# A graph network on one core: the dense rows by products of the layers' weights, on a periodic schedule, with beta added by VectorE

## The reference

```python
h = relu(layernorm(x))
x = x + L0(h)            # (h + aggregated messages) @ W0.T + b0, leaky 0.01
h = relu(layernorm(x))
x = x + L1(h)            # four attention layers, each as below
# one layer: h = x @ W; out = segment_sum(h[src] * alpha, dst) + b
#   mu, var over the row; x = (out - mu) * rsqrt(var + eps) * g + beta
```

## Time and profile before

| | |
|---|---|
| median of 3 runs | 3483.99 us (3440.52 to 3486.61) |
| profiled execution | 3488.22 us, its span 3486.5 us |
| busy share of the span | PE 64%, DVE 62%, ACT 49%, POOL 40% |
| mean granted TensorE clock | 0.677 of full |
| data moved by DMA | 126.29 MB, mean 36 GB/s |

### The profile page before, as it was taken

The page is one execution under the profiler, slowest core; times in us unless marked ns, Lnnn a source line. Parts: engine busy times, 40 slices in busy tenths (PEclk is TensorE's granted clock), DMA queues, the critical chain, the costliest instruction groups (busy, mean ns, idle before and its releaser), DMA issues. The chain is left out here.

```text
span 3486.5 us, 45031 instructions
## 1 busy us (share of the span) xinstructions
PE 2234.9 (64%) x11717; PEld 1789.5 (51%) x11717; DVE 2147.7 (62%) x8249; ACT 1723.3 (49%) x5173; POOL 1377.2 (40%) x1089
## 2 busy tenths in 40 slices
PE   2788888886546488890288891188894088797000
PEld 2666666664334366780166781166683066686000
DVE  2367776666888567448767448777446867412880
ACT  0265665554557556444566444566445456422340
POOL 5588778670112466000366000266100076200367
PEclk9976775565555566995567895566697566678555
DMA  6221222110002311000311000311000311003011
GB/s 123 59 50 32 45 67 55 31 19 15 0 0 79 102 34 26 16 1 0 107 34 26 16 1 0 106 34 26 17 1 1 96 26 42 18 1 71 3 31 37
DMA packets 101670, 126.29 MB, mean 36 GB/s; under 512 B 59443, under 2 KB 67563, under 8 KB 98091
## 3 DMA queue, kind: packets, MB, share of 16 engines
q1 hardware_dynamic: 38634, 97.42, 9.8%
q0 software_dynamic: 62400, 25.68, 4.4%
q10 hardware_dynamic: 432, 0.79, 0.1%
HBM read 78.68 MB, written 64.50 MB: 41 GB/s over the span
## 5 line engine op out<-in xcount | busy, mean ns | idle before, releaser
L227 POOL DMA_INDIRECT S<-row_t,INFG x400 | 516.5, 1291 | 1101.1 <-issue 1101.1
L221 PE MATMUL bank<-WC,XT 128*125 128x128 f32 x4800 | 845.9, 330 | 0.0
L221 PEld LDWEIGHTS bank<-WC,XT 128*125 128x125 f32 x4800 | 712.6, 227 | 172.7 <-issue 172.7
L210 PE MATMUL bank<-ident,Y 125*128 125x125 f32 x2200 | 443.7, 354 | 434.1 <-ACT Y L708 396.3
L210 PEld LDWEIGHTS bank<-ident,Y 125*128 125x128 f32 x2200 | 355.0, 189 | 481.1 <-issue 394.1
L217 PE MATMUL bank<-BR,ones 3*125 3x512 bf16 x725 | 385.1, 531 | 125.9 <-ACT XT L697 75.7
L735 DVE TENSOR_REDUCE ss<-Y 125x4 f32<-125x512 f32 x300 | 205.6, 685 | 367.6 <-ACT Y L680 367.6
L221 PE MATMUL bank<-W,XT 128*125 128x128 f32 x1200 | 310.4, 438 | 44.2 <-ACT XT L1033 44.2
L697 ACT ACTIVATE XT<-bank,BC,GC 128x500 f32<-128x500 f32 x300 | 230.3, 768 | 185.7 <-PE bank L210 185.7
L221 PEld LDWEIGHTS bank<-W,XT 128*125 128x125 f32 x1200 | 265.8, 326 | 108.5 <-issue 54.6
L217 PEld LDWEIGHTS bank<-BR,ones 3*125 3x125 bf16 x725 | 107.1, 148 | 273.8 <-ACT XT L697 118.9
(11 more groups left out here) (205 smaller groups left out, 3961.8 us busy)
## 6 DMA issues: line engine op xcount, KB each, us to landing
R<-in_x SPq DMA_DIRECT2D x100, 224.0 KB
out_rows<-R SPq DMA_DIRECT2D x100, 224.0 KB
row_t<-T SPq DMA_DIRECT2D x20, 1120.0 KB
S<-row_t,INFG POOLq DMA_INDIRECT x400
R<-in_edge_attr SPq DMA_DIRECT2D x1, 5600.0 KB
x_t<-R SPq DMA_DIRECT2D x5, 1120.0 KB
S<-x_t SPq DMA_DIRECT2D x1, 5600.0 KB
R<-in_x SPq DMA_DIRECT2D x100, 26.0 KB
```

The lines of the kernel that those rows point to most:

```text
L210: ins = nc.tensor.transpose(ps[:, a * P:(a + 1) * P], t, ident[0:P, 0:P])
L221: ins = nc.tensor.matmul(pz[0:P, a, :], xt[:, a * P:(a + 1) * P], w, start=bias is None and a == 0, stop=True, skip_group_check=True)
L227: pool.indirect_dma_start(to, None, table, bass.IndirectOffsetOnAxis(ap=idx, axis=0), bounds_check=rows - 1, oob_is_err=False).then_inc(do ...
```

## The change

**Algebra.** Before division by its root, what layer l makes of a row is linear in h0, the row that enters the first layer, and in the roots of the layers before. So the matrices are multiplied with each other once, in setup: `AC[:, l]` holds the centred weights of layer 0 times gamma times those of layer 1 and so on, and `EB` the biases that go with each root. A group is now transposed twice only (`turn1` for `W0`, `turn2` for h0). From h0 come the products with `AC[:, 0:3]`, 384 columns at once (`layers`), of which ACT takes only the mean squares (`norms`, twelve squares with an accumulator a group); six dot products a row with `PC` (`DOTS`); from these numbers DVE and ACT work out the three roots s1, s2, s3 in a chain of small instructions on 125x4 numbers; then `last_layer` (`AC[:, 3]`, four products) and `add_biases`, one matmul of thirteen rows, the roots, with `EB`.

**Schedule.** There are no rounds of five groups. In turn t each engine does a fixed list of steps, each for the group t - lag, with lags from 0 to 7; a stage of n groups has n + 8 turns. `SHARES = [68, 8, 8, 8, 8]` now counts groups. POOL's moves stand without a wait between them. Rows have twelve buffers. The add of beta is DVE's.

**Setup** makes `AC`, `PC`, `KC` and `EB`. The semaphores of the convolution stages get shared names. The attention stages are unchanged.

```diff
-SHARES = [8, 3, 3, 3, 3]
+SHARES = [68, 8, 8, 8, 8]
...
+                sp.wait_ge(s_e4, 1)
+                sp.wait_ge(s_ebz, 1)
+                for a in range(Q):
+                    for j in range(3):
+                        sp.dma_start(EB[j * Q + a:j * Q + a + 1, a * D:(a + 1) * D],
+                                     E4[j + 1:j + 2, :]).then_inc(s_eb, 16)
+                    sp.dma_start(EB[KS - 1:KS, a * D:(a + 1) * D], E4[0:1, :]).then_inc(s_eb, 16)
...
-                        if q - 8 in visit and visit[q - 8][1] == 1:
-                            pool.wait_ge(*t_done.at(nth[q - 8]))
-                            xs = rows(visit[q - 8][0])
-                            nc.gpsimd.tensor_tensor(xs, xs, B3[:, :].unsqueeze(1).broadcast_to([P, Q, D]),
-                                                    ALU.add).then_inc(beta_added.s, 1)
...
-                    for q in range(1, max(visit) + 4, 2):
-                        run(q, [(-3, product), (-2, product), (-1, transpose), (0, transpose)])
+                    for t in slots:
+                        run(t, [(5, last_layer), (3, layers(3)), (2, turn2), (5, add_biases), (0, turn1),
+                                (2, layers(0)), (2, layers(1)), (0, conv), (4, turn_s), (2, layers(2))])
...
+                    for t in slots:
+                        run(t, [(3, copy2), (6, square_last), (0, root1), (1, copy1), (2, root2),
+                                (5, s_root(2, third_sum, s3_ready)), (6, root_last),
+                                (4, s_root(0, first_sum, s1_ready)), (3, norms(0)), (3, norms(1)), (2, normalise2),
+                                (5, copy_s), (4, s_root(1, second_sum, s2_ready)), (1, slope), (0, normalise1),
+                                (3, norms(2)), (3, norms(3))])
...
+                    def add_beta(g):
+                        nc.vector.tensor_tensor(rows(g), rows(g), B3[:, :].unsqueeze(1).broadcast_to([P, Q, D]),
+                                                ALU.add).then_inc(beta_added.s, 1)
...
+                    for t in slots:
+                        run(t, [(3, normalise2), (0, statistics1), (2, leak), (5, with_s2), (2, join),
+                                (0, aggregate1), (2, statistics2), (5, times_s2), (2, aggregate2), (4, sums),
+                                (5, third), (6, sum_last), (7, multiply), (0, invert1), (6, invert_last),
+                                (2, invert2), (0, scale1), (5, fourth), (4, with_s1), (2, scale2), (4, times_s1),
+                                (0, normalise1), (4, second), (7, finish), (6, add_beta)])
```

More of the change, by code:

```diff
@@ L40 @@
 GROUPS = N // (P * Q)
-STEPS = 2 + L - 1
+XS = 12
+KS = 3 * Q + 1
 SW = 64
@@ L378, in _ @@
+                for c0 in (0, 3, 9):
+                    ch.add(nc.vector.tensor_scalar(KC[:, c0:c0 + 1], KC[:, c0:c0 + 1], EPS, None, ALU.add))
                 ch.link(nc.vector.tensor_copy(bpart[:, 0, :, :], brow))
@@ L635, in _ @@
                 def _(sp):
[L636 to L646, removed]
@@ L650, in _ @@
+                    for g in range(max(groups - XS, 0), groups):
+                        sp.wait_ge(*stored[g % XS].at(32 * (g // XS + 1)))
                 @block.tensor
                 def _(pe):
[L652 to L657, removed]
@@ new lines, in turn2, with conv @@
+                    def turn2(g):
+                        pe.wait_ge(*y2_vector.at(g + 1))
+                        pe.wait_ge(*y2_scalar.at(g + 1))
+                        if g + 1 >= 0:
+                            pe.wait_ge(*copied1.at(min(g + 2, groups)))
+                        transposes(TURN, [Y[:, 2 + g % 2, a, :] for a in range(Q)]).then_inc(turned2.s, 1)
+                    def conv(g):
+                        pe.wait_ge(*copied1.at(g + 1))
+                        if g:
+                            pe.wait_ge(*leaked.at(g))
+                        products(CONV, H1[:, g % 2, :], W0[:, :], L).then_inc(conv_done.s, 1)
@@ new lines, in h0, with last_layer, add_biases @@
+                    def h0(g, a):
+                        return XT[:, g % NS, a * P:(a + 1) * P]
+                    def last_layer(g):
+                        pe.wait_ge(*s_copied.at(g + 1))
+                        for a in range(Q):
+                            nc.tensor.matmul(last_of(g)[:, a, :], h0(g, a), AC[:, 3, :], start=a == 0, stop=False,
+                                             skip_group_check=True)
+                    def add_biases(g):
+                        nc.tensor.matmul(LAST[g % 2][0:P, :], SB[:, g % 2, :], EB[:, :], start=False,
+                                         stop=True, skip_group_check=True).then_inc(last_done.s, 1)
@@ new lines, in normalise2 @@
+                    def normalise2(g):
+                        act.wait_ge(*scaled2.at(g + 1))
+                        if g >= 2:
+                            act.wait_ge(*turned2.at(g - 1))
+                        for a in range(2):
+                            ins = nc.scalar.activation(Y[:, 2 + g % 2, a, :], rows(g)[:, a, :], ACT.Identity,
+                                                       bias=nm2[:, g % NS, a:a + 1], scale=rr2[:, g % NS, a:a + 1])
+                        ins.then_inc(y2_scalar.s, 1)
@@ L817, in gnn_kernel @@
+            mixed4.base += 2 * groups
+            for sig in (layers_done, normed):
+                sig.base += groups * Q
+            for s in range(XS):
+                loaded[s].base += 32 * ((groups - s + XS - 1) // XS)
+                stored[s].base += 32 * ((groups - s + XS - 1) // XS)
         G = C // Q
@@ L1191, in _ @@
                     (6, ln4.scale)])
+        for norm in (ln3, ln4):
+            norm.end()
+        for s in (t_done2, xt_ready2, z_done2, carried2, summed2, leaky_ready2, x1_ready2):
+            s.base += G
         s_refresh = sem("s_refreshed")
```

681 lines of the change are left out of this document (421 added, 260 removed).

## The result

The changed kernel takes 3125.3 us, median of 4 runs (3107.89 to 3183.77), the kernel before 3483.47 us, median of 4 (3440.52 to 3486.61). One of the changed kernel's four executions (3183.77 us) was a slow one and is left out of the ratio, which is 0.8981 with an interval of 0.8881 to 0.9081: faster. The prediction was 3330 us (3200 to 3470), so the direction was right and the size wrong by 205 us. The profiled execution of the changed kernel took 3135.0 us with a span of 3133.1; before, the span was 3486.5.

What follows compares the result with a forecast made beforehand. It took PE to lead before the change, with its clock at a mean of 0.69 in a later dense stage. 3488.2 + 171 (first dense stage) - 357 (later ones) + 27 (setup) = 3329, taken as 3330 us, range 3200 to 3470.

Steps and rivals of the forecast that it cites:

- The turn at full clock: Dense stages at 2.4 GHz: DVE ends last, 10.2 us plus 0.6 of waits, 10.8 us a turn.
- The doubt that the prediction named first: Dense turn, PE: `layers` taken to cost by its columns, 2.6 us at full clock; otherwise the forecast would be most wrong.
- lower bound of PE's load at half clock: Dense group on PE at 1.2 GHz: 11.5 us if a tile takes 0.44 whatever its width; 15.2 was taken.
- The clock: Dense stages: full and half clock alternate within a few turns, 70 to 30, giving 12.1 us a turn.
- Later dense stages: Four stages of eight groups: POOL's hundred gathers come last, 162 us each, 648 against 1005.5, -357 us.
- Setup: Work added ahead of the edge attributes' load: 18 us on DVE and PE, 9 on SP, together +27 us.
- Attention: Attention stages, code unchanged: 74 us at half clock could go or some 400 be lost; taken as 0.
- A: Dense stages: full clock holds and DVE bounds at 10.8 us a turn; 3240 us in all; chance 0.20.
- B: Dense stages: half clock holds and PE bounds at 15.2 us a turn; 3540 us, no change; chance 0.10.
- C: Dense stages: half clock, PE also waits for ACT's copies, 17.2 us a turn; 3724 us, slower; chance 0.07.
- D: Attention loses at its start what the clock gave, more than 90 us; up to 3500 us; chance 0.09.
- E: Later dense stages don't shrink to POOL's time, since 15 turns are not 8; 3433 us; chance 0.04.

Runs made afterwards that it cites:

- ten BATCH_NORM_STATS2: Changed kernel with ten more BATCH_NORM_STATS2 of 128 numbers, output unused, in DVE's `statistics1` of every group; turn 10.52 us, first dense stage 776.3 us.

## Why the prediction was wrong, and where it was right

- **The turn at full clock: the term that failed first.** "So when PE runs at 2.4 GHz, DVE ends last" was right. But its "10.2 us plus waits in the chain of roots", 10.8 us a turn, measured 8.5. DVE's instructions were priced by their busy time each, 0.16 us for a small one, while in a full list they start 0.04 to 0.14 us apart (0.07 in the rows after); ten BATCH_NORM_STATS2 of 0.277 us cost 2.0 us, not 2.8. By the distances between starts in the changed kernel's trace, the fifteen small ones take 1.5 us a turn in place of 2.4, beta 0.6 in place of 0.69, and all others 6.4 in place of 7.1. I had read distances between starts for PE and ACT and not for DVE. The 0.6 us of waits did not exist: DVE was busy 20.00 of 20.00 us. ACT's 9.0 was 8.25, PE's 7.8 was 8.0 at most. The doubt that the prediction named first, `layers`, was not borne out: in the kernel with fewer squares, where PE never rests, its eight matmul records of a group start 0.35 us apart, 2.8 us against 2.6, so it does cost by its columns. (The prediction's lower bound of PE's load at half clock, 11.5 us, does not follow from its terms, which give 10.4; nothing rests on it.)
- **The clock: the step that failed second.** "I expect both clocks to alternate within a few turns", 70 to 30: "That gives 0.7 x 10.8 + 0.3 x 15.2 = 12.1 us a turn." With PE loaded for some 8.0 of 8.5 us the clock was 0.92 of full over the stage, so half clock for 16% of it and not 30. (The profile's clock has its first entry at 190.93 us and counts all before as full; but PE's bias matmul took 0.68 us at 184.24 and 0.42 at 193.81, so the stage's first 30 us ran at half clock, and the share is some 20%.) Behind 411 us it cost 0.47 us a turn, 8.97 in place of 8.5. At the assumed turn itself it was 0.95 and cost nothing. The row at 1.74 of 3.41 us busy showed that the clock can fall; it could not say how often it would in a turn in which PE rests for half a microsecond. In the changed kernel it fell at 484.52 and 539.11 us, after windows of the same length in which PE was busy for 3.27 and 2.94 us. Why it fell there stays open.
- **The sum of both.** At 8.98 us in place of 12.1 a turn the first stage is 68 x 3.1 = 212 us shorter than predicted. With the right turn and the assumed shares the formula gives 0.7 x 8.5 + 0.3 x 15.2 = 10.5, so about half of the 3.1 us is the turn's and half the clock's. Filling, draining, first load and last store were 648.7 - 68 x 8.98 = 38 us against 36.
- **Later dense stages: right, 7 us each too short.** 676.4 us against 648, and POOL last as forecast, with PE idle for 51 us. A gather took 1.64 us from start to start against 1.58: two pauses of 2.2 us and a little, 1.29 us for 1.27 in the mean, since nine of the first stage's hundred gathers lasted up to 1.72 us, all of them before DVE's work ended. The second part is 2.3 us a stage, at most what the Trainium skill's rule on the shared port ("SBUF — State Buffer", "Who interferes with whom") could have cost, for which I had estimated up to 10.
- **Setup: right.** The edge attributes were issued at 54.55 us, forecast 50 to 72, and the stage grew by 21.5 us, forecast 27; 9.3 of them are the sixteen DMAs, forecast 9.
- **Attention: right by luck.** -6 us in sum, but the single stages went from 273 to 310 us with one code, by how late the clock rose. In the other runs most are at 272.3 to 273.7, so such a stage has that floor, and both profiled executions stood some 50 us above it in sum.
- **The rivals.** A (full clock holds, DVE bounds) was the nearest to what happened and got 0.20; its 3240 us used the same 10.8, and full clock held for some 80% of the stage, not all of it. B and C needed half clock over long stretches, which came at most together with ACT's remote waits; D and E did not come.

## What to carry to other kernels

Before pricing an engine's new list, read the distance between starts in a stretch where that engine never rests; busy means of isolated instructions overstated this list by a fifth. Don't average the turns of two clock levels: where another engine bounds the turn and PE has long pauses, short stretches at half clock are made up in them (turns of 10.52 and 12.41 us here); with PE as full as in the changed kernel they cost 0.47 us a turn. When the main loop has become shorter than what runs beside it, look at once at the split, since the free time beside POOL's gathers took seven more groups a stage for 5 us.

## What the runs showed of the hardware that was not expected

- A small DVE instruction with two inputs in SBUF waited for the whole of a GpSimd add: 1085 ns in the mean in place of 203.
- In the kernel without beta and with fewer squares the granted clock was 1.00 from 192 to 727 us without a fall, with eight transposes a turn among PE's matmuls; PE was busy for 523.5 of the 527 us from 200 on.
- On two chips ACT waited 7 to 27 us for something outside the core, always between 240 and 411 us, where POOL scatters into `info_t` (245 to 409 us in the changed kernel); on a third and in the changed kernel's own profile never. The kernel before with another split had none on one of these two chips. The cause stays open.
